# Norm sums as half-precision pairs on TensorE, a new start of the first call, and new tick tables, in a fused layer of feed-forward, delta-rule attention and feed-forward

## What is computed

```python
x = x + 0.5 * ffn(layernorm(x))
x = x + attn(layernorm(x))          # attn returns its own input + scan_out @ w_out + b_out
x = x + 0.5 * ffn(layernorm(x))     # the same weights as the first
# ffn:  h = silu(x@w1*s1) * (x@w2*s2);  h = gelu(h@h1);  h = gelu(h@h2);  h@w3   (1024 wide, weights -1, 0, 1)
# attn: layernorm, projections q, k, v, beta (16 heads of 16); k is divided by its norm; then for every token
#       S = S + beta*(v - S k) k^T ;  o = S q
```

## Time and profile before

| | us |
|---|---|
| median of three runs | 1684.17 |
| the profiled execution, its own time | 1685.35 |
| its span, first to last instruction | 1683.5 |
| TensorE busy in it | 1625.6 |
| GpSimd busy | 1320.1 |
| VectorE busy | 1265.6 |
| ScalarE busy | 1193.6 |
| granted TensorE clock, mean | 0.998 |

### The profile page before, as it was taken

How to read it: one execution, slowest core, us unless ns; L and a number is a source line. 1 busy time by engine, 2 the same in 40 slices (tenths; PEclk the granted TensorE clock), 3 DMA queues, 4 the chain that set the end, 5 groups by cost and what they waited for, 6 DMA issues and landing times.

```text
span 1683.5 us, 32506 instructions
## 1 busy us (share of the span) xinstructions
PE 1625.6 (97%) x10897; PEld 986.9 (59%) x10897; DVE 1265.6 (75%) x3152; ACT 1193.6 (71%) x2302; POOL 1320.1 (78%) x1658
## 2 busy tenths in 40 slices
PE   6989999999999999999999999999999999999989
PEld 4865555565655555555656565555556565555668
DVE  5456878878788878788787888787887878887531
ACT  4667777777777787777777777877777777775744
POOL 5574988878787979888787879798887878796743
PEclk9999999999999999999999999999999999999999
DMA  8100000000010000100010000001000000000000
GB/s 310 47 3 5 3 4 4 4 5 4 3 29 4 5 4 3 29 4 5 4 29 3 5 4 4 4 3 29 4 4 4 4 3 17 4 17 4 16 1 14
DMA packets 74917, 27.55 MB, mean 16 GB/s; under 512 B 70272, under 2 KB 71296, under 8 KB 73216
## 3 DMA queue, kind: packets, MB, share of 16 engines
q1 hardware_dynamic: 74752, 25.47, 5.7%
HBM read 17.06 MB, written 4.19 MB: 13 GB/s over the span
## 4 chain that ended last, share of the span: by engine, by line
PE 67%; DVE 11%; POOL 8%; ACT 8%; issue 7%; DVEq 0%; ACTq 0%; POOLq 0%
PE ffn_bank L1188 43%; PE att_bank L1209 6%; PE ffn_bank L1171 4%; POOL hid_lo L628 3%; DVE hid L932 3%; PE att_bank L1224 2%; PE att_bank L1139 2%; PE att_bank L1225 2%; DVE terms L1034 2%; ACT state_parts L818 2%; PE att_bank L1258 2%; PE att_bank L1238 2%; PE state_bank L1249 2%; POOL pairs L657 2%; POOL pairs_lo L665 1%
## 5 line engine op out<-in xcount | busy, mean ns | idle before, releaser
L1188 PE MATMUL ffn_bank<-hid_hi,w_sb 128*128 128x448 f16 (+1 forms) x2880 | 942.4, 337 | 5.1 <-POOL hid_lo L628 3.6
L1188 PE MATMUL ffn_bank<-hid_lo,w_sb 128*128 128x448 f16 (+1 forms) x2880 | 942.2, 337 | 0.0
L628 POOL TENSOR_TENSOR hid_lo<-hid,hid_hi 128x448 f16<-128x448 f32 (+1 forms) x480 | 460.6, 978 | 139.4 <-ACT hid_hi L745 122.3
L657 POOL TENSOR_TENSOR pairs<-KQ 128x32 f32<-128x32 f32 (+15 forms) x496 | 337.3, 697 | 143.6 <-DVE KQ L960 140.3
L1188 PEld LDWEIGHTS ffn_bank<-hid_hi,w_sb 128*128 128x128 fp8e4 x2880 | 285.0, 99 | 201.6 <-issue 7.7
L1188 PEld LDWEIGHTS ffn_bank<-hid_lo,w_sb 128*128 128x128 fp8e4 x2880 | 282.4, 98 | 203.9 <-issue 9.8
L665 POOL TENSOR_TENSOR pairs_lo<-pairs,pairs_hi 128x448 f16<-128x448 f32 (+15 forms) x416 | 305.8, 748 | 14.0 <-ACT pairs_hi L832 14.0
L745 ACT CAST hid_hi<-hid 128x448 f16<-128x448 f32 (+1 forms) x480 | 238.9, 534 | 58.3 <-DVE hid L932 56.5
L832 ACT CAST pairs_hi<-pairs 128x448 f16<-128x448 f32 (+15 forms) x416 | 178.1, 441 | 113.4 <-POOL pairs L657 112.1
L1171 PE MATMUL ffn_bank<-xn_hi,w_sb 128*128 128x448 f16 (+1 forms) x640 | 211.9, 340 | 23.7 <-DVE hid L932 15.7
L769 ACT ACTIVATE hid<-ffn_bank,par_sb 128x448 f32<-128x448 f32 (+1 forms) x320 | 174.8, 597 | 70.1 <-PE ffn_bank L1188 69.0
(11 more groups left out here) (96 smaller groups left out, 2159.3 us busy)
## 6 DMA issues: line engine op xcount, KB each, us to landing
NK<-in_w SPq DMA_DIRECT2D x11, 1024.0 KB, 6.9
Kz<-KTr SPq DMA_DIRECT2D x256, 16.0 KB, 1.9
X<-in_x SPq DMA_DIRECT2D x7, 512.0 KB, 3.6
out<-X SPq DMA_DIRECT2D x7, 512.0 KB, 2.9
wqkvb_sb<-in_wqkvb SPq DMA_DIRECT2D x1, 1024.0 KB, 8.8
X<-in_x SPq DMA_DIRECT2D x2, 256.0 KB, 6.7
out<-X SPq DMA_DIRECT2D x2, 256.0 KB, 2.1
wout_sb<-in_wout SPq DMA_DIRECT2D x1, 256.0 KB, 9.4
```

The lines of the kernel that those rows point to most:

```text
L628: pool.tensor_tensor(hid_lo[layer % 2][:, m, 0:call.width], hid[:, u % HID_BUFFERS, 0:call.width], hid_hi[layer % 2][:, m, 0:call.width], ...
L657: pool.tensor_tensor(packed(pair(pairs, q, dot), n), later, earlier, ALU.mult).then_inc(pairs_made if dot in SPLIT else pairs_ready, 1)
L1188: mm = nc.tensor.matmul(ffn_ps(call, j), weight(name, kk, 2 * pair + i), v[:, kk, cols], start=kk == 0 and part == 0, stop=kk == KT_FF - 1 ...
```

## The change

1. Every norm job but the first: behind `sum`, ScalarE copies `feature_sum` to f16 (`sum_high`), GpSimd subtracts to get the f16 rest (`sum_low`), and the `mean` matmul in f32 becomes two f16 matmuls with an f16 matrix of 1/256, high part and low part, into one bank. The same for `sq_sum` and `var` (`sq_high`, `sq_low`). The parts lie in the half of `roots` that is free at that time. Four new semaphores order this. One more 128x128 memset sets the f16 matrix.
2. The first call: the eleven weight conversions on VectorE are placed otherwise. The first moves between `center` and `recip` of the first norm; between the gatings there are two (after the fourth and the sixth `mix`) in place of four; two follow behind the eighth.
3. All tick tables and lags are set anew.

```diff
-E_RETR = [1, 22, 45, 67]
-E_STATE = [17, 39, 58, 81]
-E_PROJ = {K_: 40, Q_: 54, V_: 52, B_: 40}
+E_RETR = [0, 24, 45, 66]
+E_STATE = [18, 42, 60, 84]
+E_PROJ = {K_: 42, Q_: 51, V_: 47, B_: 48}
 E_NORM = 44
-E_OUT = 57
-E_QK = [1, 11, 5, 14, 3, 7, 11, 29, 21, 22, 36, 32, 30, 43, 40, 54]
+E_OUT = 56
+E_QK = [3, 15, 7, 24, 16, 14, 12, 33, 28, 44, 34, 34, 28, 48, 43, 53]
-E_KK = dict(zip(KK_ROWS, [56, 57, 63, 64, 66, 66, 66, 73, 75, 84, 82, 86, 83, 87, 60]))
-PAIR_LEAD = {"whole": 12, "half": 11}
+E_KK = dict(zip(KK_ROWS, [56, 61, 59, 63, 57, 64, 66, 72, 80, 83, 83, 85, 86, 87, 80]))
+PAIR_LEAD = {"whole": 10, "half": 13}
-ACT_LAG, POOL_LAG, DVE_LAG = 1, 4, 1
-SPLIT_LAG, SPREAD_LAG = 2, 4
-E_KQ_HIGH, E_K_LOW, E_Q_LOW = 67, 68, 77
+ACT_LAG, POOL_LAG, DVE_LAG = 1, 6, 0
+SPLIT_LAG, SPREAD_LAG = 1, 2
+E_KQ_HIGH, E_K_LOW, E_Q_LOW = 57, 73, 60
-TURN_LEAD, U_HIGH_LEAD, U_LOW_LEAD = 5, 3, 3
+HEAD_CONVERTS = (3, 5)
+TURN_LEAD, U_HIGH_LEAD, U_LOW_LEAD = 6, 4, 1
-    return dict(sum=at + 2, mean=at + 5, center=at + 4, square=at + 7, sq_sum=at + 7, var=at + 11, root=at + 10, recip0=at + 14, recip1=at + 15, recip2=at + 17, recip3=at + 19, norm=at + 19, apply=at + 21, low=at + 20)
+    return dict(sum=at, sum_high=at, sum_low=at + 1, mean=at + 5, center=at + 3, square=at + 4, sq_sum=at + 6, sq_high=at + 8, sq_low=at + 10, var=at + 13, root=at + 9, recip0=at + 10, recip1=at + 13, recip2=at + 18, recip3=at + 19, norm=at + 19, apply=at + 21, low=at + 22)
-LN_ATT = dict(sum=11, mean=15, center=18, square=17, sq_sum=26, var=26, root=25, recip=30, norm=39, y_recip=39, apply=40, low=44)
-LN_FFN = 64
+LN_ATT = dict(sum=10, sum_high=7, sum_low=10, mean=11, center=10, square=14, sq_sum=17, sq_high=17, sq_low=20, var=24, root=24, recip=28, norm=35, y_recip=41, apply=38, low=42)
+LN_FFN = 65
-SAVE_LAG = 1
+SAVE_LAG = 2
@@ gpsimd
+                if part == "sum_low" and i:
+                    pool.wait_ge(sum_hi_ready, i)
+                    pool.tensor_tensor(sum_parts[:, 1, 0:n], feature_sum[:, cols], sum_parts[:, 0, 0:n], ALU.subtract).then_inc(sum_lo_ready, 1)
@@ scalar
+                if part == "sum_high" and i:
+                    act.wait_ge(ln_summed, i + 1)
+                    act.copy(sum_parts[:, 0, 0:n], feature_sum[:, cols]).then_inc(sum_hi_ready, 1)
@@ vector, alone()
-                    for part in ("center", "recip", "norm"):
-                        ln(part, job)
+                    ln("center", job)
+                    convert(0)
+                    ln("recip", job)
+                    ln("norm", job)
                 if second:
-                    for i in range(2):
-                        convert(i)
-                    for i in range(2, 2 + KT_FF // 2):
-                        mix(call, 2 * i - 4)
-                        mix(call, 2 * i - 3)
-                        convert(i)
+                    convert(1)
+                    for m in range(KT_FF):
+                        mix(call, m)
+                        if m in HEAD_CONVERTS:
+                            convert(2 + HEAD_CONVERTS.index(m))
+                    convert(4)
+                    convert(5)
@@ tensor
-                    nc.tensor.matmul(ps[:, 0:cols.stop - cols.start], average[:, :], feature_sum[:, cols], start=True, stop=True).then_inc(att_filled, 1)
+                    if i:
+                        nc.tensor.matmul(ps[:, 0:n], average16[:, :], sum_parts[:, 0, 0:n], start=True, stop=False)
+                        nc.tensor.matmul(ps[:, 0:n], average16[:, :], sum_parts[:, 1, 0:n], start=False, stop=True).then_inc(att_filled, 1)
+                    else:
+                        nc.tensor.matmul(ps[:, 0:n], average[:, :], feature_sum[:, cols], start=True, stop=True).then_inc(att_filled, 1)
```

More of the change, by code:

```diff
@@ L172 @@
 QUARTERS = 4
-TURN_LEAD, U_HIGH_LEAD, U_LOW_LEAD = 5, 3, 3
+HEAD_CONVERTS = (3, 5)
+TURN_LEAD, U_HIGH_LEAD, U_LOW_LEAD = 6, 4, 1
 def ffn_ln(at):
-    return dict(sum=at + 2, mean=at + 5, center=at + 4, square=at + 7, sq_sum=at + 7, var=at + 11, root=at + 10, recip0=at + 14, recip1=at + 15, recip2=at + 17, recip3=at + 19, norm=at + 19, apply=at + 21, low=at + 20)
+    return dict(sum=at, sum_high=at, sum_low=at + 1, mean=at + 5, center=at + 3, square=at + 4, sq_sum=at + 6, sq_high=at + 8, sq_low=at + 10, var=at + 13, root=at + 9, recip0=at + 10, recip1=at + 13, recip2=at + 18, recip3=at + 19, norm=at + 19, apply=at + 21, low=at + 22)
 def half_ln(at):
-    return dict(sum=at + 5, mean=at + 2, center=at + 3, square=at + 8, sq_sum=at + 5, var=at + 7, root=at + 9, recip0=at + 9, recip1=at + 9, recip2=at + 11, recip3=at + 12, norm=at + 13, apply=at + 13, low=at + 14)
-LN_ATT = dict(sum=11, mean=15, center=18, square=17, sq_sum=26, var=26, root=25, recip=30, norm=39, y_recip=39, apply=40, low=44)
-LN_SECOND = dict(sum=25, mean=22, square=29, sq_sum=31, var=43, root=42, apply=58, low=63)
-LN_FFN = 64
+    return dict(sum=at, sum_high=at + 1, sum_low=at + 2, mean=at + 3, center=at + 4, square=at + 5, sq_sum=at + 6, sq_high=at + 7, sq_low=at + 8, var=at + 9, root=at + 10, recip0=at + 10, recip1=at + 11, recip2=at + 12, recip3=at + 13, norm=at + 14, apply=at + 15, low=at + 16)
+LN_ATT = dict(sum=10, sum_high=7, sum_low=10, mean=11, center=10, square=14, sq_sum=17, sq_high=17, sq_low=20, var=24, root=24, recip=28, norm=35, y_recip=41, apply=38, low=42)
+LN_SECOND = dict(sum=21, sum_high=30, sum_low=31, mean=34, square=30, sq_sum=36, sq_high=33, sq_low=37, var=42, root=33, apply=54, low=60)
+LN_FFN = 65
 JOBS = []
@@ L589, in ln @@
                 i, cols = job.i, job.cols
-                total = feature_sum[:, cols].unsqueeze(1)
+                total, n = feature_sum[:, cols].unsqueeze(1), cols.stop - cols.start
                 if part == "sum":
@@ L611, in ln @@
                     pool.tensor_tensor(total, xn[:, 0:1, cols], xn[:, 1:2, cols], ALU.add).then_inc(ln_sq_summed, 1)
+                if part == "sum_low" and i:
+                    pool.wait_ge(sum_hi_ready, i)
+                    pool.tensor_tensor(sum_parts[:, 1, 0:n], feature_sum[:, cols], sum_parts[:, 0, 0:n], ALU.subtract).then_inc(sum_lo_ready, 1)
+                if part == "sq_low" and i:
+                    pool.wait_ge(sq_hi_ready, i)
+                    pool.tensor_tensor(sum_parts[:, 1, 0:n], feature_sum[:, cols], sum_parts[:, 0, 0:n], ALU.subtract).then_inc(sq_lo_ready, 1)
                 if part == "low" and job.kind != "att":
@@ L720, in ln @@
                 n = cols.stop - cols.start
+                if part == "sum_high" and i:
+                    act.wait_ge(ln_summed, i + 1)
+                    act.copy(sum_parts[:, 0, 0:n], feature_sum[:, cols]).then_inc(sum_hi_ready, 1)
+                if part == "sq_high" and i:
+                    act.wait_ge(ln_sq_summed, i + 1)
+                    act.copy(sum_parts[:, 0, 0:n], feature_sum[:, cols]).then_inc(sq_hi_ready, 1)
                 if part == "square":
```

21 lines of the change are left out of this document (16 added, 5 removed).

## The result

The changed kernel takes 1726.25 us (median of 4 runs, 1725.13 to 1726.41) beside 1684.93 us for the kernel before on the same chip: ratio 1.0239, 95% interval 1.0226 to 1.0251. It is slower by 41 us, and outside the forecast's range. Its span is 1723.4 us, 39.9 us over before's 1683.5.

What follows compares the result with a forecast made beforehand. TensorE was taken to bound the frame, with VectorE second in the gating stretch and GpSimd from `key_norm` on. Frames -16, head -2, frame -1 +1, remaining frames -2 gave -19 us: 1665 us, forecast 1655 to 1676, range 1645 to 1686.

## What to carry to other kernels

When an edit adds work to GpSimd, or moves it, look at every VectorE instruction with two SBUF inputs for the length of GpSimd's run that it will meet (here that gave an upper bound: beside the same run it took 1.37 us or 3.52), and read the price from VectorE's records, not from GpSimd's. Where such an instruction is on the path, a wait that makes GpSimd stand aside for it can be worth more than it costs (here 35 us). And an engine at 78% busy may be full where the path goes through it: added time there has to be set against every wait that its queue feeds, not one.

## What the runs showed of the hardware

A VectorE product of 512 columns with both inputs in SBUF takes 0.69 us alone, and in the changed kernel and two versions of it 3.52, 2.48 or 1.41 us, as GpSimd has three, two or one instructions before its next gap. In isolation, beside GpSimd runs of six instructions without a gap, it never took over 1.73 us; it also got in between two of them in the kernel before (at 427.24) and in the new order with f32 sums (at 518.97, 1.37 us). In both the next GpSimd instruction was then the longer one (1.12 us in place of 0.67, 1.54 in place of 1.10). The 896-column product of the changed kernel met the same neighbours in every frame and came out both ways, 2.12 us in six frames and 1.13 in nine. What makes the difference was tried (waits, shapes, ScalarE's casts, a PSUM product ahead) and not found; it stays open. A product with one input in PSUM took 0.69 us beside the same runs, and a reciprocal its 3.35 us.
